# Attention value products: four column groups of 32 at once, both halves of cross-attention summed in one bank, one turning back per attention

## The reference

```python
x = _layernorm(x + _L0_attn_ref(x, Wqkv_w, Wqkv_b, out_w, out_b))     # 16 heads of 16, ONE key and value head, causal
x = _layernorm(x + _L0_xattn_ref(x, ctx_512, ctx_512))                # 32 heads of 8, 8 key/value heads of 8
x = _layernorm(x + _L0_ffn_ref(x, ...))                               # base part, and 2 of 8 experts per token
...
scores = jnp.einsum('bqhd,bkd->bhqk', q, k) * scale                   # self-attention
ctx = jnp.einsum('bhqk,bkd->bqhd', softmax(masked scores), v)
...
scores = jnp.einsum('bkgsd,bktd->bkgst', qh, kh) / scale              # cross-attention
out = jnp.einsum('bkgst,bktd->bkgsd', softmax(scores), vh)
```

## Time and profile before

| what | value |
|---|---|
| median of 3 runs | 708.4 us (706.02 to 711.39) |
| the profiled execution, its own time | 704.1 us |
| its span, first to last instruction | 701.9 us |
| mean granted TensorE clock over the span | 0.957 of full speed |
| busy: PE, PEld, DVE, ACT, POOL | 89%, 61%, 65%, 48%, 20% |
| length of a complete step (3 to 11) | 21.21 us |

### The profile page before, as it was taken

One profiled execution on the slowest core, in us unless ns is written; L12 is line 12 of the kernel. 1 busy time (PEld: TensorE's weight loads), 2 busy tenths in 40 slices (PEclk: granted clock), 3 DMA queues, 4 the chain that ended last, 5 costly groups with the idle time before them and its releaser, 6 DMA issues. The chain is left out here.

```text
span 701.9 us, 11383 instructions
## 1 busy us (share of the span) xinstructions
PE 627.2 (89%) x3351; PEld 425.6 (61%) x3379; DVE 458.5 (65%) x1020; ACT 333.9 (48%) x705; POOL 142.7 (20%) x159
## 2 busy tenths in 40 slices
PE   2767999999999999999887798999999999999981
PEld 2444455555455555555433576888888788887770
DVE  3479889888988888988764583344343344344296
ACT  2355777777777777776744311132322232223114
POOL 2033110111110111110100002143433343341000
PEclk9889999999999999999968799999999999999996
DMA  8104443324443234443320681016436653110703
GB/s 263 36 1 158 157 158 128 105 102 163 166 166 131 82 119 165 165 159 121 135 98 14 230 331 31 16 53 214 170 120 223 224 165 108 47 52 19 239 1 120
DMA packets 54440, 90.47 MB, mean 129 GB/s; under 512 B 6284, under 2 KB 25231, under 8 KB 54384
## 3 DMA queue, kind: packets, MB, share of 16 engines
q1 hardware_dynamic: 50640, 80.43, 33.2%
q0 software_dynamic: 3744, 9.31, 4.2%
HBM read 56.18 MB, written 34.47 MB: 129 GB/s over the span
## 5 line engine op out<-in xcount | busy, mean ns | idle before, releaser
L1169 ACT ACTIVATE silu<-inner 128x512 f32<-128x512 f32 x55 | 32.9, 598 | 159.7 <-PE inner L1550 110.6
L486 ACT ACTIVATE prob<-scores 128x1024 f32<-128x1024 f32 x96 | 98.4, 1027 | 13.0 <-PE scores L859 8.6
L1329 DVE TENSOR_TENSOR hT<-hiddenT,hT 128x512 fp32r<-128x512 f32 x39 | 27.0, 692 | 87.9 <-ACT hT L1175 87.9
L632 DVE TENSOR_REDUCE max_c<-scores 128x8 f32<-128x1024 f32 x64 | 78.0, 1218 | 8.8 <-PE scores L922 7.2
L1545 PE MATMUL inner<-weights,sT_hi 128*128 x156 | 68.7, 440 | 0.3
L946 PE MATMUL sums<-prob,v_c 128*32 128x512 f32 x256 | 66.9, 648 | 0.0
L1135 POOL DMA_INDIRECT chosen_y<-lane_hot,to_row x39 | 40.0, 1026 | 132.2 <-DVE lane_hot L1344 132.2
L1546 PE MATMUL inner<-weights,sT_hi 128*128 x156 | 61.5, 394 | 0.0
L398 POOL TENSOR_TENSOR xT_lo<-xT_in,xT_hi 128x256 fp32r<-128x256 f32 x16 | 11.9, 745 | 236.1 <-ACT xT_hi L457 236.1
L1129 POOL DMA_INDIRECT rows<-x,from_row x39 | 38.2, 979 | 87.8 <-DVE from_row L1311 76.2
L932 PE MATMUL scores<-q_c,k_c 128*128 128x512 f32 x128 | 46.5, 445 | 5.9 <-ACT prob L486 2.8
(11 more groups left out here) (218 smaller groups left out, 1430.0 us busy)
## 6 DMA issues: line engine op xcount, KB each, us to landing
split_w<-halves SPq DMA_DIRECT2D x32, 768.0 KB, 5.3
weights<-split_w SPq DMA_DIRECT2D x8, 3072.0 KB, 12.8
raw_w<-in_expert_w SPq DMA_DIRECT2D x16, 768.0 KB, 4.6
weights<-chosen_y SPq DMA_DIRECT2D x8, 512.0 KB, 7.5
xT_in<-in_xT SPq DMA_DIRECT2D x16, 128.0 KB, 4.6
x_in<-in_x SPq DMA_DIRECT2D x16, 128.0 KB, 3.6
x<-stream SPq DMA_DIRECT2D x16, 128.0 KB, 4.6
ctxT_in<-in_ctxT SPq DMA_DIRECT2D x16, 96.0 KB, 4.0
```

Of the source, the lines that this page charges most:

```text
L486: act.activation(prob[:, m, :], scores[:, n, :], ACT.Exp, scale=scale).then_inc(sem[exped], 1)
L632: dve.tensor_reduce(out_[:, 8 * unit:8 * unit + 8], scores[:, n, :].rearrange("p (h k) -> p h k", k=S), AX.X, ALU.max).then_inc(sem[read], 1)
```

## The change

The value products are made four at a time. Self-attention's values take 32 columns (v_s is 128 x 32 where it was 128 x 64), and its one remaining s_sum makes all four products (2 halves of heads x 2 units) on the four column groups, into one bank. Cross-attention's c_sum now covers two units: unit a makes four products on the four column groups. Its two calls go to the same bank, the second added to the first; for this the values of the second half lie 16 columns further (v_c is 128 x 288, function `value_places`), so that each group of 32 result rows has the first half's in rows 0 to 8 and the second half's in rows 16 to 24, with zeros added elsewhere. One copy to SBUF, one turning back with four transposes and one reciprocal per attention are left where there were two; the multiplications stay two per attention. The tables are written anew, with fewer entries and some in other places.

```diff
 PE_ORDER = [
...
-    ("c_sum", 1, -1), ("s_main", 1, 2), ("c_shift", 0, 0), ("c_sum", 2, -1), ("s_max", 0, 3), ("c_sum", 3, -1),
...
+    ("c_sum", 0, -1), ("s_main", 1, 2), ("c_shift", 0, 0), ("s_max", 0, 3), ("c_sum", 1, -1),
...
-PROB_USE = {"s_exp": ("s_summed", 2), "c_exp": ("c_summed", 4)}
-SUM_USE = {"s_sum": ("s_sum_read", 2), "c_sum": ("c_sum_read", 2)}
+PROB_USE = {"s_exp": ("s_summed", 1), "c_exp": ("c_summed", 2)}
+SUM_USE = {"s_sum": ("s_sum_read", 1), "c_sum": ("c_sum_read", 1)}
 MISC_USE = {
...
-    "s_out": [("s_ctx", 2, None)],
+    "s_out": [("s_ctx", 1, 1)],
...
-    "c_out": [("c_ctx", 2, None)],
+    "c_out": [("c_ctx", 1, 1)],
...
-            prob.append((stage, unit, 0, delta, name, per, unit + 1))
+            prob.append((stage, unit, 0, delta, name, per, unit // 2 + 1))
...
-        v_s = two("v_s", [P, 64])
+        v_s = two("v_s", [P, 32])
...
-        v_c = two("v_c", [P, 2, 128])
+        v_c = two("v_c", [P, 2 * 144])
...
+        def value_places(v):
+
+            return v[:].rearrange("p (a c) -> p a c", a=2)[:, :, 0:128].rearrange("p a (j s) -> p a j s", j=4)
...
-                act.copy(sumT_s[:, unit, :], sums[:, n, :]).then_inc(sem["s_sum_read"], 1)
+                act.copy(sumT_s[:], sums[:, n, :]).then_inc(sem["s_sum_read"], 1)
...
-                act.copy(sumT_c[:, a, :], sums[:, n, :]).then_inc(sem["c_sum_read"], 1)
+                act.copy(sumT_c[:], sums[:, n, :]).then_inc(sem["c_sum_read"], 1)
...
+                dve.reciprocal(rden_c[:], misc[:, n, :].rearrange("p (m s) -> p m s", s=16)[:, :, XD:XD + 1].squeeze(2))\
...
-            def s_sum(seq, b):
-
-                p, n, m = seq.odd, sum_ring.slot("s_sum", b, seq), prob_ring.slot("s_exp", b, seq)
-                wait(pe, sem["s_exp"], seq, 2, b + 1)
+            def s_sum(seq, unit):
+
+                p, n = seq.odd, sum_ring.slot("s_sum", 0, seq)
+                wait(pe, sem["s_exp"], seq, 2)
                 wait(pe, sem["s_rows_hi"], seq)
-                sum_ring.wait_free(pe, sem, "s_sum", b, seq)
+                sum_ring.wait_free(pe, sem, "s_sum", 0, seq)
                 for h in range(2):
-                    mm = pe.matmul(sums[64 * h:64 * h + 64, n, :], v_s[p][:], prob[:, m, 512 * h:512 * h + 512], start=True, stop=True)
+                    for b in range(2):
+                        at = 64 * h + 32 * b
+                        mm = pe.matmul(sums[at:at + 32, n, :], v_s[p][:], prob[:, prob_ring.slot("s_exp", b, seq), 512 * h:512 * h + 512],
+                                       start=True, stop=True)
                 mm.then_inc(sem["s_summed"], 1)
...
-            def c_sum(seq, unit):
-
-                p, a, m = seq.odd, unit // 2, prob_ring.slot("c_exp", unit, seq)
-                n = sum_ring.slot("c_sum", 2 * a, seq)
-                wait(pe, sem["c_exp"], seq, 4, unit + 1)
+            def c_sum(seq, a):
+
+                p, n = seq.odd, sum_ring.slot("c_sum", 0, seq)
+                wait(pe, sem["c_exp"], seq, 4, 2 * a + 2)
                 wait(pe, sem["ctx_v_set"], seq)
-                if unit % 2 == 0:
-                    sum_ring.wait_free(pe, sem, "c_sum", unit, seq)
-                for v in range(2):
-                    j = 2 * (unit % 2) + v
-                    mm = pe.matmul(sums[32 * j:32 * j + 32, n, :], v_c[p][:, a, 32 * j:32 * j + 32], prob[:, m, 512 * v:512 * v + 512],
-                                   start=True, stop=True)
+                if a == 0:
+                    sum_ring.wait_free(pe, sem, "c_sum", 0, seq)
+                for j in range(4):
+                    m, v = prob_ring.slot("c_exp", 2 * a + j // 2, seq), j % 2
+                    mm = pe.matmul(sums[32 * j:32 * j + 32, n, :], v_c[p][:, P * a + 32 * j:P * a + 32 * j + 32],
+                                   prob[:, m, 512 * v:512 * v + 512], start=(a == 0), stop=(a == 1))
                 mm.then_inc(sem["c_summed"], 1)
```

More of the change, by code:

```diff
@@ L55 @@
     ("s_proj", 0, 1), ("c_max", 2, 0), ("s_main", 0, 2), ("s_turn", 0, 3), ("c_max", 3, 0), ("s_res", 0, 1),
[L56 to L59 removed]
+    ("c_sum", 0, -1), ("s_main", 1, 2), ("c_shift", 0, 0), ("s_max", 0, 3), ("c_sum", 1, -1),
+    ("c_main", 0, 0), ("c_main", 1, 0), ("c_out", 0, -1), ("s_max", 1, 3),
+    ("c_turn", 0, 1), ("c_main", 2, 0), ("c_max", 0, 1), ("s_qkv", 0, 4), ("s_sum", 0, 2),
+    ("s_shift", 0, 3), ("c_main", 3, 0), ("s_out", 0, 2), ("c_max", 1, 1),
     ("x2_logit", 0, -3), ("x2_turn", 0, -2),
@@ L69 @@
 DVE_ORDER = [
-    ("s_den", 1, 1), ("s_out", 1, 1), ("c_max", 1, 0), ("s_rows", 0, 3), ("s_proj", 0, 1),
+    ("s_den", 0, 1), ("s_out", 0, 1), ("c_max", 1, 0), ("s_rows", 0, 3), ("s_proj", 0, 1),
     ("c_max", 2, 0), ("c_aggr", 0, -2), ("c_keys", 0, 1), ("s_turn", 0, 3), ("c_max", 3, 0),
@@ L183, in rings @@
             score.append((stage, unit, 0, delta, name, per, unit + 1))
-        if stage == "s_sum" or stage == "c_sum" and unit % 2 == 0:
+        if stage in SUM_USE and unit == 0:
             name, per = SUM_USE[stage]
-            summed.append((stage, unit, 0, delta, name, per, (unit if stage == "s_sum" else unit // 2) + 1))
+            summed.append((stage, unit, 0, delta, name, per, 1))
         for part, (name, per, upto) in enumerate(MISC_USE.get(stage, [])):
@@ L466, in s_rows @@
                 wait(act, sem["s_k_full"], seq.back(1))
-                wait(act, sem["s_summed"], seq.back(2), 2)
+                wait(act, sem["s_summed"], seq.back(2))
                 q = qkv[:, 0:D].rearrange("p (n c) -> p n c", c=32)
@@ L494, in s_read @@
             def s_read(seq, unit):
-                n = sum_ring.slot("s_sum", unit, seq)
-                wait(act, sem["s_summed"], seq, 2, unit + 1)
-                wait(act, sem["s_out_full"], seq.back(1), 2, unit + 1)
-                act.copy(sumT_s[:, unit, :], sums[:, n, :]).then_inc(sem["s_sum_read"], 1)
+                n = sum_ring.slot("s_sum", 0, seq)
+                wait(act, sem["s_summed"], seq)
+                wait(act, sem["s_out_full"], seq.back(1))
+                act.copy(sumT_s[:], sums[:, n, :]).then_inc(sem["s_sum_read"], 1)
             def c_read(seq, a):
-                n = sum_ring.slot("c_sum", 2 * a, seq)
-                wait(act, sem["c_summed"], seq, 4, 2 * a + 2)
-                wait(act, sem["c_out_full"], seq.back(1), 2, a + 1)
-                act.copy(sumT_c[:, a, :], sums[:, n, :]).then_inc(sem["c_sum_read"], 1)
+                n = sum_ring.slot("c_sum", 0, seq)
+                wait(act, sem["c_summed"], seq, 2)
+                wait(act, sem["c_out_full"], seq.back(1))
+                act.copy(sumT_c[:], sums[:, n, :]).then_inc(sem["c_sum_read"], 1)
             def s_proj(seq, unit):
@@ L874, in turn_sums @@
                 n = misc_ring.slot(stage, unit, seq)
-                wait(pe, sem[read], seq, 2, unit + 1)
+                wait(pe, sem[read], seq)
                 misc_ring.wait_free(pe, sem, stage, unit, seq)
                 for j in range(4):
-                    mm = pe.transpose(misc[:, n, S * j:S * j + S], source[:, unit, S * j:S * j + S], ident[:])
+                    mm = pe.transpose(misc[:, n, S * j:S * j + S], source[:, S * j:S * j + S], ident[:])
                 mm.then_inc(sem[full], 1)
@@ L888, in s_proj @@
                 n = misc_ring.slot("s_proj", 0, seq)
-                wait(pe, sem["s_ctx"], seq, 2)
+                wait(pe, sem["s_ctx"], seq)
                 misc_ring.wait_free(pe, sem, "s_proj", 0, seq)
```

82 lines of the change are left out of this document (42 added, 40 removed).

## The result

The changed kernel took 754.99 us, median of four runs (744.68 to 758.26), beside 707.21 for the kernel before on the same chip (705.58 to 711.39). The ratio is 1.062, with a 95% interval of 1.050 to 1.074; ratios go by the fast runs alone, and the one of 758.26 is not among them. On another chip it was 753.85 beside 703.62, 1.070 (1.065 to 1.075). The forecast was 714.9, with a range of 699 to 728.

What follows compares the result with a forecast made beforehand. TensorE was taken to bound the kernel, busy 20.67 of a 21.21 us step. Waits adding 0.8 us in 13 steps (+10.4), less 2.9 and 1 at the ends, gave +6.5 on 708.4: 714.9 us, range 699 to 728.

Steps and rivals of the forecast that it cites:

- Do four cost what two cost?: Joined value-product calls on TensorE: yes, 0.98 us on the queue for four products; 1.96 if the bank made them take turns.
- The 0.3 more a call: Skill page's counter-estimate for joined value products: some 0.3 us longer each, 0.6 a step, about 8 in all, giving 722.
- What is removed: Per step: TensorE loses 4.0 us of value products and turnings; ScalarE two copies of 0.59; VectorE two reciprocals, at most 0.25 each.
- First wait, prob for s_exp0: s_exp0 needs the slot that c_sum0 frees, directly before s_main1: TensorE stands 1.2 us there.
- Second wait, scores for c_main1: c_main1 needs the scores slot read by s_max0's maximum: TensorE stands about 1 us, using up everything gained so far.
- Third wait, prob for c_exp2: c_exp2 needs the slot freed by the joined s_sum: starts at 17.56 us instead of 14.86, making the step 22.0.
- the second rival: Chain of waits right but half a microsecond shorter: step 0.2 to 0.3 us longer than before, kernel 708; chance 0.18.
- The sum: Whole kernel: 13 steps at 0.8 give 10.4 us, the end steps -2.9 and -1, together +6.5.
- The price is 22.0 - 21.2 = 0.8 us a step: Complete attention step, s_proj to s_proj: 22.0 us after the change against 21.2 before.
- The clock: Rival: TensorE's waits for c_exp2 and s_read halve its clock in every second step, 11 us on top, 726; chance 0.22.
- the forecast's likeliest case: Whole kernel: 709 to 722 us, with chance 0.50.
- First rival, VectorE as the bound: Waits are covered and VectorE bounds the step: 19.4 us a step, -23 in all, about 685; chance 0.10.

Runs made afterwards that it cites:

- six slots: The changed kernel with 6 slots of prob instead of 4, tables as they are: 682.1 us, ratio 0.970 to the kernel before.
- the kernel with filled stands and a narrow sum on POOL: The changed kernel with unread products before s_main1, c_main1, c_main3 and s_out, and POOL's x_bias sum one column wide instead of 256: 724.6 us, 1.024.
- the kernel with filled stands: The changed kernel with unread bf16 products in TensorE's waits before s_main1 (5), c_main1 (7), c_main3 (4) and s_out (2): 726.8 us, 1.033.
- the late filling: The changed kernel with unread products only before c_main3 (4) and s_out (2): 728.9 us, 1.034.
- either half of the filling: The changed kernel with unread products only before c_main3 and s_out (728.9 us), or only before s_main1 and c_main1 (747.1 us).

## Why the prediction was wrong

*Do four cost what two cost?* Right. The joined calls take 1.06 and 1.07 us at full clock, against the 1.05 and 1.08 of the earlier trace rows. That they go to one bank costs nothing that these rows show. The 0.3 more a call, worked out from the Trainium skill (TensorE: Matmul & The Clock Gate, Measured speedup vs the span model), does not show in these rows. (By its own figures that estimate is 723, not 722.)

*What is removed.* TensorE's work came out at 17.1 us a step (six slots, full clock), where 16.7 was forecast, and VectorE's at 18.42, where 18.1 was. One reciprocal of both halves is longer than one of a half, 0.35 against 0.25 in cross-attention, so that only part of two reciprocals went.

*First wait, prob for s_exp0.* Right: PE stands 1.29 us before line 866, where 1.2 was forecast, and ACT 2.21. Only the handing over was mis-sized: ACT's exponential starts 1.19 after the start of a call of eight records (206.47, 207.66), not 1.10.

*Second wait, scores for c_main1.* The place is right, and the size not: 1.69 in after, where about 1 was forecast. 0.5 of it is VectorE behind POOL. The forecast took VectorE's instructions at their lengths of before, each in the place that the step now gave it, and did not ask what POOL does at that time.

*Third wait, prob for c_exp2.* Right in place and in its chain. In the kernel with filled stands and a narrow sum on POOL, where neither clock nor POOL disturbs, s_sum lies 16.92 behind s_proj (forecast 16.46), c_exp2 18.12 (17.56), and the next s_proj 22.47 (22.0). The 0.47 between them came in small pieces, most from handings over that were each taken a tenth too short: 0.08 up to c_sum0, 0.09 to s_exp0, 0.09 to s_main1, 0.10 from there to c_main1, 0.10 to s_sum, 0.09 to c_exp2, and 0.09 given back behind it. That was the second rival with its sign turned around: the chain was longer by half a microsecond, not shorter.

*The sum.* The step that failed on the waits is "The price is 22.0 - 21.2 = 0.8 us a step": at full clock it is 22.97 less 21.21, 1.8, of which 0.5 is POOL and 0.5 the joints. Thirteen steps of 1.8 are 23.4, and the kernel with filled stands is 23.4 slower than before. That the two agree is partly luck: in the traces it is +0.7 up to the first s_proj, +27.5 from there to the last, and -4.8 behind it. The sum of the forecast was 6.5.

*The clock.* This is the step that decided. The rival named a cause (PE stands for c_exp2 and for s_read within 3 us) and the likeness to the earlier trace rows, and the late filling shows that cause to be the larger part of it; the two earlier stands, which the rival left out, have a share too. Wrong were its chance, 0.22, and its price: "If that happens in every second step, 0.85 x 13 = 11". It costs 27 us, the difference between the kernel and the one with filled stands; over nine steps it is 231.05 less 207.90, 2.6 a step where 0.85 was priced. The chain of the forecast itself contained the two stands, 0.9 and 0.7, and the earlier trace rows gave what such a stretch does. The clock was in the steps of the forecast's likeliest case, and yet was counted as a case apart from it. Why the price came out so much larger can be read from the steps. From step 1 on they last 22.57, 23.5, 28.48, 25.22, 24.6, 24.32, 26.73, 24.32, 28.36 us at clocks 1.00, 0.98, 0.74, 0.84, 0.92, 0.92, 0.82, 0.92, 0.74. At 0.74 a step is 5.5 us longer than at full clock: half clock then holds for about half the step, not for the 3.4 us that were priced.

The Trainium skill (TensorE: Matmul & The Clock Gate, HAM oscillation) describes waits for DMA that bring the clock down at each turn of a loop. Here waits for other engines do so in eight of these nine steps of after; with six slots, where there is a stand in each step too, the clock stays at 1.00 in nine steps.

*First rival, VectorE as the bound.* It did not happen with four slots and did with six: 19.59 a step where 19.4 was worked out, and 682 us where 685 was. But the 685 is 23 less than 708.4, and the 682 is 21 less than 703.4.

*What stays open.* The kernels show which stands matter here, not what a stand must be for the clock to fall. A step whose only stand of more than half a microsecond was one of 1.21 left the clock at 1.00; stands of 0.40, 0.77 and 0.23 with short work between them let it fall in some steps and not in others. Nor is it known why either half of the filling gives back so much alone that the two shares add up to more than the whole. The kernel before with six slots was not run; only the bound above stands for it.

## What to carry to other kernels

When two units of work are joined, the call frees the buffers of both at the later time, and a ring that was just deep enough becomes the bound: here two more slots turned 1.07 into 0.97. Where a forecast puts new stands of TensorE close together, the fall of the clock belongs in the sum and not among the rivals, as it came with them in eight of nine steps here, and unread products put into the stands measure what it costs. When a chain is shifted in time, look at what the other engines do at its new time.

## What the hardware showed that was not expected

**TensorE works more and the kernel is faster.** Eighteen unread products a step saved 27 us, and six in the right places nearly as much. Here it counts more where TensorE stands than how much it works in a step: at 17.1 busy of 19.6 us with one long stand the clock was 1.00; at 17.0 of 19.6 with three late ones the next step ran at 0.92.

**A one-column instruction of VectorE can be held by POOL for POOL's whole length.** In the profiled execution of after it is t_s as well (DVE, then POOL):

```profile
187.63 0.76 DVE L729 SCALAR_TENSOR_TENSOR t_s<-t_s,r_s 128x1 f32<-128x1 f32 x1
...
187.64 0.73 POOL L424 TENSOR_TENSOR x_bias<-x_in,b_o 128x256 f32<-128x256 f32 x1
```

Both end together, at 188.39 and 188.37; alone, the instruction takes 0.16. The Trainium skill (SBUF — State Buffer, SBUF: two separate sides) says that VectorE with two inputs in SBUF and GpSimd share a pair of ports as an exclusive lock, and that the loser blocks for the whole instruction. The rows agree: the delay is POOL's remaining time, though VectorE's own operand has one column. The two records begin 0.01 apart, so they don't tell which of the two had the ports first. VectorE's tensor_scalar of line 717 (210.22) ran wholly inside POOL's sum of before (209.79 to 210.53) and took its usual 0.21, so not every small instruction is held.
